# A four-layer gated attention stack on one core: layer 4's 128 attention units written out, values read from their own buffer

## What is computed

```python
N_HEADS = 32; HEAD_DIM = 128; N_KV_HEADS = 4; N_GROUPS = 8
hidden_states = jnp.concatenate([context, latents], axis=1)        # 128 + 128 keys
q = (latents @ Wq).reshape(b, q_len, N_KV_HEADS, N_GROUPS, HEAD_DIM)
k = (hidden_states @ Wk).reshape(b, kv_len, N_KV_HEADS, HEAD_DIM)
v = (hidden_states @ Wv).reshape(b, kv_len, N_KV_HEADS, HEAD_DIM)
scores = jnp.einsum('bqhgd,bkhd->bhgqk', q, k) * scale
attn = jax.nn.softmax(scores, axis=-1)
out = jnp.einsum('bhgqk,bkhd->bqhgd', attn, v)
return out.reshape(b, q_len, N_HEADS * HEAD_DIM) @ Wo
...
x = x + jnp.tanh(g_xattn[3]) * _L3_xattn_ref(_layernorm(x), ctx_4096, ...)
```

## Time and profile before

| | us |
|---|---|
| median of 3 runs | 2828.01 |
| lowest, highest | 2826.79, 2834.16 |
| the profiled execution | 2830.24 |
| its span, first to last instruction | 2828.4 |

### The profile page before, as it was taken

One profiled execution on the slowest core, in us unless ns is written; L12 is line 12 of the kernel. 1 busy time (PEld: TensorE's weight loads), 2 busy tenths in 40 slices (PEclk: granted clock), 3 DMA queues, 4 the chain that ended last, 5 costly groups with the idle time before them and its releaser, 6 DMA issues.

```text
span 2828.4 us, 45548 instructions
## 1 busy us (share of the span) xinstructions
PE 2714.3 (96%) x14480; PEld 2269.5 (80%) x14480; DVE 1744.0 (62%) x3407; ACT 1116.0 (39%) x3084; POOL 828.0 (29%) x707
## 2 busy tenths in 40 slices
PE   6997999999999998899999999899999999999998
PEld 5885788888888887677888888678878888888886
DVE  4756645545545546587999999745444555555557
ACT  3542333333333333135666666421124444434442
POOL 4002333333333332323222222155522212222200
PEclk8998999999999999999999999999999999999999
DMA  5001111111111111111111101021211100000000
GB/s 147 14 5 62 38 38 45 37 37 44 37 38 44 38 37 37 39 34 38 34 33 31 33 31 33 23 56 57 56 45 34 31 24 27 27 28 27 27 5 30
DMA packets 59805, 106.17 MB, mean 38 GB/s; under 512 B 7184, under 2 KB 11536, under 8 KB 59536
## 3 DMA queue, kind: packets, MB, share of 16 engines
q1 hardware_dynamic: 56448, 96.49, 12.2%
q10 hardware_dynamic: 3216, 7.81, 0.8%
HBM read 100.09 MB, written 2.10 MB: 36 GB/s over the span
## 4 chain that ended last, share of the span: by engine, by line
PE 90%; DVE 6%; ACT 2%; issue 1%; DMA 0%; POOL 0%; ACTq 0%; DVEq 0%; POOLq 0%
PE four L608 50%; PE outp L608 24%; PE value L608 9%; PE turned L957 4%; PE turned L730 1%; DVE stats L1611 1%; DVE xt_lo L1640 0%; DVE x L1848 0%; PE turned L655 0%; DVE nt L1739 0%; DVE probs L1753 0%; DVE x L2054 0%; PE value L655 0%; ACT vc L1231 0%; DVE probs L1635 0%
## 5 line engine op out<-in xcount | busy, mean ns | idle before, releaser
L579 POOL TENSOR_TENSOR w_hi<-raw,zero 128x512 fp32r<-128x512 f32 x347 | 372.6, 1074 | 1849.4 <-PE four L608 628.9
L1848 DVE SCALAR_TENSOR_TENSOR x<-outp,g_inv,x 128x512 f32<-128x512 f32 x768 | 552.6, 748 | 388.8 <-PE outp L608 388.1
L583 POOL TENSOR_TENSOR w_lo<-raw,w_hi 128x512 fp32r<-128x512 f32 x352 | 453.9, 1290 | 32.1 <-ACT w_hi L1231 4.9
L608 PE MATMUL four<-xt_hi,w_lo 128*128 128x512 f32 x1024 | 429.4, 419 | 10.4 <-DVE xt_lo L1640 10.4
L608 PE MATMUL four<-xt_hi,w_hi 128*128 128x512 f32 x1024 | 404.7, 395 | 0.0
L608 PE MATMUL four<-xt_lo,w_hi 128*128 128x512 f32 x1024 | 403.7, 394 | 0.0
L608 PE MATMUL outp<-w_hi,a_lo 128*128 128x512 f32 x800 | 326.4, 408 | 18.6 <-DVE a_lo L1944 9.6
L608 PE MATMUL outp<-w_hi,a_hi 128*128 128x512 f32 x800 | 317.1, 396 | 0.0
L608 PE MATMUL outp<-w_lo,a_hi 128*128 128x512 f32 x800 | 315.9, 395 | 0.0
L1231 ACT ACTIVATE pT<-turned 128x512 f32<-128x512 f32 x320 | 192.7, 602 | 238.7 <-PE turned L957 180.8
L1436 ACT ACTIVATE probs<-probs,top 128x128 f32<-128x128 f32 x512 | 199.6, 391 | 210.2 <-DVE top L1892 125.9
(11 more groups left out here) (275 smaller groups left out, 4525.6 us busy)
## 6 DMA issues: line engine op xcount, KB each, us to landing
raw<-in_stream SPq DMA_DIRECT2D x352, 256.0 KB, 2.6
ctx_raw<-in_ctx_t ACTq DMA_DIRECT2D x4, 512.0 KB, 6.2
x<-in_x_in ACTq DMA_DIRECT2D x2, 1024.0 KB, 11.6
kz<-kT SPq DMA_DIRECT2D x32, 64.0 KB, 2.7
pb<-in_position_bias ACTq DMA_DIRECT2D x1, 2048.0 KB, 8.2
out<-x SPq DMA_DIRECT2D x8, 256.0 KB, 2.0
qw<-in_qweight ACTq DMA_DIRECT2D x1, 768.0 KB, 3.8
ln_w<-in_ln_weight ACTq DMA_DIRECT2D x1, 256.0 KB, 3.0
```

The source lines that it names most:

```text
L579: pool.tensor_tensor(w_hi[:, k, :], raw[:, k % RAW, :], zero[:, :].to_broadcast([P, D]), ALU.add)\
L583: pool.tensor_tensor(w_lo[:, k, :], raw[:, k % RAW, :], f32(w_hi[:, k, :]), ALU.subtract)\
L608: m = pe.matmul(out_, l, r, start=start, stop=stop, skip_group_check=True)
L1848: dve.scalar_tensor_tensor(out=x[:, b, :], in0=O[no_f(k) % 2][:, :], scalar=scale, in1=x[:, b, :], op0=ALU.mult, op1=ALU.add)\
```

## The change

The loop of L3 goes: with a period of 0, `run_steps` writes all 130 steps out on PE, ACT and DVE. Every semaphore target and every index of L3 is then a constant. The four copies into `vc` go from ACT, and with them the semaphore; `values` loads the same 128 columns for each sequence from `v`, at the column offset of its head. For its first unit it waits until `v` is written. The buffer `vc3` keeps its place. POOL and SP, and the layers before, are as they were.

```diff
 ATT = [Narrow(), Attention("L1", HEADS, 2, 8),
-       Attention("L2", HEADS, 2, 8), Attention("L3", HEADS, 4, 32)]
+       Attention("L2", HEADS, 2, 8), Attention("L3", HEADS, 4, 0)]
...
                         else:
-                            kv = at(L, lambda i: i // L.U // 8, k, it)
-                            keys = buf["kT"][:, kv, b, :] if it is None else \
-                                buf["kT"][:, bass.ds(kv, 1), b, :].rearrange("p a k -> p (a k)")
+                            keys = buf["kT"][:, h // 8, b, :]
...
-                    else:
-                        per = 4 if n == 2 else 8
-                        pe.wait_ge(s["vc"], at(L, lambda i: i // L.U // per + 1, k, it))
+                    elif n == 2:
+                        pe.wait_ge(s["vc"], at(L, lambda i: i // L.U // 4 + 1, k, it))
+                    elif k == 0:
+                        pe.wait_ge(s["j_out"], max(L.evac[("Vc", 0, B - 1)], L.evac[("Vx", 0, B - 1)]))
...
                             else:
-                                v = buf["vc"][:, kt, b, :]
+                                v = buf["v"][:, kt, b, tokens(h // 8)]
...
-                    per = {2: 4 * L.U, 3: 8 * L.U}.get(n, 0)
-                    if per and k % per == 1 and k < L.NU:
+                    per = 4 * L.U
+                    if n == 2 and k % per == 1 and k < L.NU:
...
-                        if n == 2:
-                            copy(buf["vc"][:, :, :], buf["v"][:, :, cols]).then_inc(s["vc"], 1)
-                        else:
-                            copy(buf["vc"][:, :, :, :].rearrange("p a b d -> p (a b) d"),
-                                 buf["v"][:, :, :, :].rearrange("p a b d -> p (a b) d")[:, :, cols])\
-                                .then_inc(s["vc"], 1)
+                        copy(buf["vc"][:, :, :], buf["v"][:, :, cols]).then_inc(s["vc"], 1)
```

## The result

| | before | changed |
|---|---|---|
| median of 4 runs | 2828.56 us | 2811.03 us |
| lowest, highest | 2826.79, 2834.16 | 2809.59, 2812.07 |
| the profiled execution, its span | 2830.24, 2828.4 | 2812.07, 2810.2 |

The ratio is 0.9932, with a 95% interval from 0.9918 to 0.9946: 0.68% faster, where 0.52% was forecast. So the direction held; the forecast was short by 2.8 us if the medians are compared (17.5 us), by 4.5 if the ratio is (19.2 of 2828), and the first question is where these come from.

What follows compares the result with a forecast made beforehand. PE, busy 2714.3 of 2828.4 us, was taken as the bound. Copies (5.01) plus ways back (9.76) plus 0 for straight code made 14.77 us, from the median 2828.01 to 2813.2; range 2809.5 to 2820.

Steps and rivals of the forecast that it cites:

- part 3: Layer 4's 96 looped steps as straight code, stationary operand from `v`: taken as 0, pace 1.0 us up or down.
- Part 1: Layer 4's four copies into `vc`: 2.37 us in step 1 plus 2.64 for three in the loop, together 5.01.
- Part 2: Layer 4's two ways back at the loop's end: 4.83 and 4.93 us, together 9.76; lower end 6.0, the stalls alone.
- the third shows what that copy costs alone: Gap ending layer 4's last iteration, branch not taken: 0.88 us for the copy; the first two gaps held 5.71 and 5.81.
- The price of the branch from the notes: Compare-and-branch at about 108 ns: two ways back worth 0.2 us, whole change 5.2; the measured 3.00 us was preferred.
- The first (the stall comes from fetching and moves elsewhere): PE still waits for a code block once in each former iteration; only 5.0 us go, giving 2823.0 us; 7%.
- the second (late blocks in straight code): In the 96 formerly looped steps, some 26 blocks could each stall PE 3.0 us; all late gives 2891 us; 3%.
- the third (slower loads from `v`): Layer 4's 1024 loads from `v` slower than from `vc`: 14 ns each eats the gain, 28 gives 2842 us; 2%.

Runs made afterwards that it cites:

- second comparison: The changed kernel run again, with no edit, against the kernel before: ratio 0.9945 (0.9931 to 0.9959), median 2813.76 us of 6 runs.

## Why the prediction was right and wrong

**What bounds the kernel.** Right: PE, and in layer 4 its waits for the copies and the two stalls. Apart from these only the pace of a unit changed. The list of waits has two more kinds that the prediction leaves out: 1.6 us for `a_lo` in the last two steps, which stayed, and 6.0 for `probs` behind the layer.

**The sum for the layer.** 14.77 us forecast, 15.62 measured in the layer. The step that was mis-sized is part 3, "I take 0" for the pace, to which it allowed 1.0 us up or down. The changed kernel runs all units at 4.973 us, a pace that the kernel before showed in its second iteration alone; 87 intervals in the other stretches by 0.010 are 0.87, which is the difference of 0.85. The row with 4.973 was read and taken for a spread around nothing. What sets the pace was not found: the order of matmuls is the same, other engines keep their offsets to PE within 0.02 us, and the same straight code has 4.983 when the copies are in it. Where it lies can be read by averaging the distances between starts in the kernel before: the six 128x512 matmuls of the query projection take 1469 ns together in the first iteration and 1459 in the second, and the other 22 of a unit 3514 in both. The same two values stand in four other profiles. All straight or looped stretches of layer 4 that no stall of PE in the layer precedes had 4.973, and of those behind a stall only the second iteration of the kernel before did, in both of its profiles. This is a pattern and not a cause.

**Part 1, the copies.** Right for the three in the loop (0.88 each, once they stand away from the branch) and for the change's own effect in step 1: step 1 takes 3.70 us after, 6.05 before, 2.35 less for 2.37 forecast. Short in one respect: in half of the profiles with the copy the clock falls behind it, for 1.6 us more.

**Part 2, the ways back.** The sum was right and the reason wrong. The step that failed is "the third shows what that copy costs alone, and the difference what the way back costs". The two don't add: with both, the layer takes 640.4 us; with the copies gone alone 628.1; with the loop gone alone 632.8; with both gone 624.8. A way back costs 1.0 to 1.6 us, and 4.8 to 4.9 (once 6.0) if a late wait stands right ahead of it, since then its branch and its 3 us of fetch begin late, and at each of these four longer idles the clock fell too. As both went, the sum came out whatever the split between them; it is no proof of the reasoning. The copies alone were put at 5.0 by the same reading, and without them the layer is 12.3 us shorter. The loop alone was put at 9.8 and gave 7.6, or 9.2 without the clock's fall in step 1; that is near the forecast, because it was taken out of the kernel in which the late wait makes the ways back dear. With the copies gone, taking out the loop as well is worth 3.3 us (628.1 to 624.8), under the 6.0 that stood as the lower end of part 2.

**The price of the branch from the notes.** The Trainium skill's 108 ns (Advanced Engine Details and Errata, Control Flow Timing) was set aside for the row of 3.00 us. The body of 16 steps shows when a figure of that order holds: where the target is at hand the branch takes 0.215 us in PE's sequencer, twice the page's figure, and a way back costs nothing that PE shows.

**Rivals.** The first (the stall comes from fetching and moves elsewhere), the second (late blocks in straight code) and the third (slower loads from `v`) are all out, by PE's 620.00 of 620.00 us and by the 192 ns.

**The range.** By the ratio, 0.9932, the result lies 0.7 us below the range. Of the 4.5 us beyond the forecast 0.85 are the pace, which the sum put at nothing. The second comparison doesn't have the other 3.6, so they are taken for chance between runs, of which the profiled pair shows 3.2 ahead of layer 4, and for which the range allowed 1.2. Its low end was drawn from the spread of three runs of before, 1.2 us below their median. 23 runs of the kernel before lie from 2822.4 to 2835.1, and the part ahead of layer 4 alone moves by 4.6 us between profiles. The interval of the first ratio, 0.0014 to either side, is 4 us; the forecast less that is 2809.2, and with the pace 2808.4. The second comparison, 0.9945, is 15.6 us of 2829.7, the layer's own 15.62; applied to 2828.0 it gives 2812.5, inside the range.

## What to carry to other kernels

Before two stalls that stand next to each other are priced apart, ask whether one keeps the instruction stream from running ahead: a semaphore that comes late right ahead of a loop's branch turns a mostly hidden fetch into an idle of 3 us. Move such a wait away from the branch (8 steps brought 6.4 of the 15.6 us here), or make the body short enough that its code stays, before writing the whole loop out. Look at the branch's own row in PE's sequencer: its duration tells whether the target was at hand, its start whether a wait held it. And a change of half a per cent is read from the length of the touched stage, which repeated within 0.05 us here, not from the totals of a few runs.

## What the runs showed of the hardware

- A loop body of 16 steps (by estimate four to five blocks of 16 KB of PE code) ran seven times; after the first time no block was fetched, and PE had no idle time. One of 32 steps was fetched again in each iteration, and still ran at full pace between its ends.
- A taken branch to code that isn't at hand takes 3.4 to 3.8 us in PE's sequencer (eight ways back), one to kept code 0.21 to 0.24 (the loops of layers 2 and 3, and this one with 16 steps), one not taken 0.08. The fetch comes 1.0 us behind the branch's start, and from the fetch to the first matmul behind the branch pass 2.6 to 3.2 us, whether PE has work queued meanwhile or not.
- At the first way back PE's sequencer reached the branch 1.8 us ahead of the start of the last `values` where nothing held it, and 0.2 behind it where `values` waited for `vc`.
- After idles of 2.1 us the granted clock fell to the lower level (1.2 GHz) in two profiles of four; at idles of 0.6 and 2.9 to 3.3 us with one `values` between them, each of four times. At idles of 0.7 to 1.3 us it stayed at 2.4 GHz. In layer 4 a fall lasted 3.4 us, once 6.8, and cost about 1.6 us per 3.4.
- A unit of identical matmuls has two paces, 4.973 and 4.983 us, that hold for dozens of units and repeat from execution to execution; the difference lies in the six matmuls of the query projection, 1469 or 1459 ns together. The cause is open.
